# Second-attention steps as one row over all batches, with the first attention's tiles in denser rounds

## What is computed

```python
# layer 1: 16 heads of 16
q, k, v = split(x @ w_in.T + b_in)
att = softmax(einsum('blhd,bmhd->blmh', q, k) / 4, axis=2)
opt = einsum('blmh,blhd->blhd', att, v)          # att is summed over m: only its sums and maxima matter
x = layernorm(x + opt @ w_out.T + b_out)
# layer 2: 4 of 16 heads of 64, chosen per batch
dist = softmax(mean(x @ Wr + br, axis=1))
idx = sort(top_k(dist, 4))
Q, K, V = heads idx of x @ Wq + bq, x @ Wk + bk, x @ Wv + bv
O = softmax(Q K^T / 8) V
x = layernorm(x + O @ Wo + bo)
```

## Time and profile before

| | |
|---|---|
| median of 3 runs | 4088.38 us (4088.38 to 4088.68) |
| the profiled execution | 4086.6 us |
| its span | 4084.8 us |
| PE, DVE, ACT, POOL busy | 89%, 80%, 76%, 41% of the span |
| mean granted TensorE clock | 0.887 of full speed |

### The profile page before, as it was taken

The page is one execution under the profiler, slowest core; times in us unless marked ns, Lnnn a source line. Parts: engine busy times, 40 slices in busy tenths (PEclk is TensorE's granted clock), DMA queues, the critical chain, the costliest instruction groups (busy, mean ns, idle before and its releaser), DMA issues.

```text
span 4084.8 us, 41654 instructions
## 1 busy us (share of the span) xinstructions
PE 3616.2 (89%) x13992; PEld 1329.7 (33%) x13992; DVE 3287.2 (80%) x3352; ACT 3098.1 (76%) x5069; POOL 1662.8 (41%) x1115
## 2 busy tenths in 40 slices
PE   7888888778999999788999999788999999599997
PEld 3233223223333333323333332323333322343443
DVE  7888888988989898888989898888989898543442
ACT  5888888886888889786888889786888889423333
POOL 3122332100445555400445545401445545437776
PEclk7777777678999999878999999778999999799998
DMA  5122221110000000210000000210000000100000
GB/s 159 67 75 67 83 75 62 57 45 16 16 16 19 21 21 26 67 38 16 16 16 19 26 16 26 73 33 16 16 16 25 21 16 19 53 9 1 11 11 11
DMA packets 117192, 142.62 MB, mean 35 GB/s; under 512 B 33394, under 2 KB 100466, under 8 KB 116978
## 3 DMA queue, kind: packets, MB, share of 16 engines
q1 hardware_dynamic: 116978, 139.95, 11.0%
HBM read 89.55 MB, written 50.33 MB: 34 GB/s over the span
## 4 chain that ended last, share of the span: by engine, by line
PE 47%; DVE 29%; ACT 17%; issue 5%; POOL 2%; SPq 1%; DMA 0%; POOLq 0%; DVEq 0%; ACTq 0%
DVE nmax L1083 18%; ACT ps L920 14%; PE ps L796 8%; PE ps L886 8%; PE ps L858 7%; PE ps L761 7%; PE ps L873 7%; DVE smax L1162 6%; PE ps L775 6%; POOL facc L720 2%; PE ps L876 2%; PE ps L769 1%; PE ps L894 1%; ACT probs L990 1%; DVE st L1062 1%
## 5 line engine op out<-in xcount | busy, mean ns | idle before, releaser
L920 ACT ACTIVATE ps<-ps,nmax 128x1024 f32<-128x1024 f32 x2048 | 2233.0, 1094 | 388.4 <-DVE nmax L1083 365.6
L1083 DVE TENSOR_REDUCE nmax<-ps 128x1 f32<-128x1024 f32 x2048 | 2379.4, 1216 | 135.2 <-PE ps L796 122.5
L796 PE MATMUL ps<-stack 96*128 96x512 bf16 x4096 | 1350.6, 436 | 237.0 <-ACT ps L920 149.4
L720 POOL TENSOR_TENSOR facc<-facc,probs 128x1024 f32<-128x1024 f32 x448 | 1051.2, 2346 | 550.9 <-ACT probs L990 528.8
L1162 DVE TENSOR_REDUCE smax<-ps 128x2 f32<-128x1024 f32 x512 | 616.5, 1220 | 261.3 <-PE ps L858 260.9
L796 PEld LDWEIGHTS ps<-stack 96*128 96x128 bf16 x4096 | 298.2, 102 | 1411.0 <-ACT ps L920 939.2
L990 ACT ACTIVATE probs<-ps 128x1024 f32<-128x1024 f32 x512 | 524.0, 1024 | 229.1 <-PE ps L876 227.8
L858 PE MATMUL ps<-fk,fq 64*128 64x512 f32 x2048 | 571.0, 650 | 41.4 <-ACT ps L920 38.1
L873 PE MATMUL ps<-fq,fk 64*128 64x512 f32 x2048 | 545.7, 609 | 29.0 <-ACT ps L920 27.9
L886 PE MATMUL ps<-probs,vals 128*64 128x512 f32 x2048 | 506.9, 608 | 5.0 <-ACT probs L990 4.5
L920 ACT ACTIVATION_READ_ACCUMULATOR ps<-ps,nmax 128x1 f32 x2048 | 417.0, 204 | 0.0
(11 more groups left out here) (117 smaller groups left out, 1985.5 us busy)
## 6 DMA issues: line engine op xcount, KB each, us to landing
stack<-qk_levels SPq DMA_DIRECT2D x768, 64.0 KB, 2.2
qk_levels<-fk SPq DMA_DIRECT2D x64, 384.0 KB, 2.6
probs<-in_L_attn_x SPq DMA_DIRECT2D x16, 512.0 KB, 3.8
res<-in_L_attn_x SPq DMA_DIRECT2D x16, 512.0 KB, 4.0
v_rows<-vals SPq DMA_DIRECT2D x16, 512.0 KB, 2.6
vrows<-v_rows SPq DMA_DIRECT2D x16, 512.0 KB, 3.4
x_rows<-y SPq DMA_DIRECT2D x16, 512.0 KB, 2.9
res<-x_rows SPq DMA_DIRECT2D x16, 512.0 KB, 3.9
```

The costliest lines, as they stand in the source:

```text
L720: pool.tensor_tensor(total, total, probs[:, slot, :], ALU.add).then_inc(facc_ready, 1)
L796: last = pe.matmul(bank(banks[i]), stack[0:SK, hd % 2, 0, t * P:(t + 1) * P], stack[0:SK, hd % 2, 1, col:col + CH], start=True, stop=True)
L920: act.activation(src, src, ACT.Exp, bias=nmax[:, b % 2, half, t, hd:hd + 1], scale=-1.0, accum_out=esum[:, b % 2, half, t, hd:hd + 1]).the ...
L1083: dve.tensor_reduce(nmax[:, b % 2, half, t, hd:hd + 1], two_banks(banks), AX.XY, ALU.min).then_inc(min_ready, 1)
```

## The change

The second attention's steps are numbered over all batches, so that they make one row of rounds: 32 for each batch and 4 behind the last. S of the first group of a batch stands in the same rounds as T and V of the last group of the batch before it. In the last batch those first four rounds' T and V get spots within the seam. A round takes 16 tiles (the pattern `16`) as long as more tiles are left than 12 for each round that remains, less EARLY = 48, and up to 12 otherwise; where tiles are left no more, a letter A is skipped. FK, FV and FQ of the second pair stand in a batch's first four rounds.

What follows from it for the buffers: the last chunk of foT lies in oT and no longer in x1T, and J of two batches on, and R, wait for its users; ACT's eviction of X1 waits for FK, FQ and FV of the batch before, that of FK for T of the last group that reads the same columns of fk, DVE's eviction of FV for V of that group step by step, no longer for its last; the slots of probs are counted over all batches; the norm of a batch's last FO follows the OP norms of the next batch.

The planner's prices are changed too.

```diff
-ROUND = "TSSTAASTAASTAAAVVAAVAVAA"
-LEAD = "SAAAASAAAASAAAASAAAA"
+EARLY = 48
+ROUNDS = {0: "TSSTSTSTVVVV", 12: "AASTAASTSATASTAAAVVAAVAV", 16: "STAASTAASTAASTAAAVAVAAVAAVAA"}
+LEAD = "SAAAASAAAASAAAASAAAATTTTVVVV"
...
+    near = AHEAD / A_TILES
+    rounds = GROUPS * STEPS // BURST
+    behind = STEPS // BURST
+
+    def spot_of(r, part):
+        b, k = divmod(r, rounds)
+        if b == B:
+            return B + (k + part) / rounds
+        return b + near + (1 - near) * (k + part) / rounds
...
-        later = [("FK", b, 1, c) for c in range(NCH)] + [("FQ", b, 1, 0)] + [("FV", b, c) for c in range(NCH)]
-        main += place(later, b + near, (1 - near) * STEPS / (GROUPS + 1) / STEPS)
...
+        later = [u for c in range(NCH) for u in (("FK", b, 1, c), ("FV", b, c))] + [("FQ", b, 1, 0)]
+        late += [(spot_of(b * rounds + behind * (i + 1) / len(later), 0.0), u) for i, u in enumerate(later)]
+        main += [(spot_of(b * rounds + behind * g - behind / 2, 0), ("FQ", b, g % PAIRS, g // PAIRS)) for g in range(2, GROUPS)]
+    given = [AHEAD] * B
+    for r in range(B * rounds + behind):
+        b, k = divmod(r, rounds)
+        if r < behind or b == B - 1 and k < behind:
+            spots = LEAD
+        elif b + 1 < B:
+            spots = ROUNDS[16 if A_TILES - given[b] > 12 * (rounds - k) - EARLY else 12]
+        else:
+            spots = ROUNDS[0]
+        take = {"S": r * BURST, "T": r * BURST - STEPS, "V": r * BURST - STEPS}
+        for i, kind in enumerate(spots):
+            spot = spot_of(r, i / len(spots))
+            if kind == "A":
+                if b + 1 < B and given[b] < A_TILES:
+                    tiles.append((spot, ("A", b + 1, given[b])))
+                    given[b] += 1
+                continue
...
+            if kind != "S" and b == B - 1 and k < behind:
+                spot = b + near * (k + i / len(spots)) / behind
...
-    return [main, scores, products, inputs, tiles]
+    return [main, scores, products, inputs, tiles, late]
...
-            fill(("A", b, j), 0.46, 2, [sp("LS", b, j // HEAD_TILES)] if j % HEAD_TILES == 0 else [], act("A", b, j))
-            unit(dve("A", b, j), 1.155, [pe("A", b, j)])
+            fill(("A", b, j), 0.437, 2, [sp("LS", b, j // HEAD_TILES)] if j % HEAD_TILES == 0 else [], act("A", b, j))
+            unit(dve("A", b, j), 1.135, [pe("A", b, j)])
...
-                fill(("S",) + t, 0.96, 2, [act("FK", b, p, n % NCH), dve("FQ", b, p, c)], dve("S", *t))
-                unit(dve("S", *t), 1.22, [pe("S", *t)] + ([dve("M", *two)] if two and n == 0 else []))
-                fill(("T",) + t, 1.28, 2, [act("M", b, g)] if n == 0 else [], act("T", *t))
+                fill(("S",) + t, 0.86, 2, [act("FK", b, p, n % NCH), dve("FQ", b, p, c)], dve("S", *t))
+                unit(dve("S", *t), 1.135, [pe("S", *t)] + ([dve("M", *two)] if two and n == 0 else []))
+                fill(("T",) + t, 1.17, 2, [act("M", b, g)] if n == 0 else [], act("T", *t))
...
-            events.append((now + (0.18 if n[0] == "PE" else 0.1) + extra[n], 1, r, n))
+            events.append((now + (0.1 if n[0] == "PE" else 0.05) + extra[n], 1, r, n))
...
-        foT = x1T
+        def foT(c):
+            return oT[:, :, :] if c + 1 == NCH else x1T[:, :, c * CH:(c + 1) * CH]
+
...
                     if b:
-                        act.wait_ge(filled, fill_no["FO", b - 1, c])
+                        act.wait_ge(filled, max([fill_no[k, b - 1, p, c] for k in ("FK", "FQ") for p in range(PAIRS)]
+                                                + [fill_no["FV", b - 1, c]]))
+                        if c + 1 < NCH:
+                            act.wait_ge(filled, fill_no["FO", b - 1, c])
...
+                    if b:
+                        act.wait_ge(filled, fill_no["T", b - 1, GROUPS - PAIRS + p, c * TPC + TPC - 1])
...
-                        dve.wait_ge(pv_done, step_no(b - 1, GROUPS - 1, STEPS - 1))
+                        dve.wait_ge(pv_done, step_no(b - 1, GROUPS - 1, c * TPC + TPC - 1))
...
+                    if c + 1 == NCH and b + 1 < B:
+                        dve.wait_ge(filled, fill_no["OP", b + 1, NCH - 1])
```

More of the change, by code:

```diff
@@ L41 @@
 AHEAD = 70
-ROUND = "TSSTAASTAASTAAAVVAAVAVAA"
-LEAD = "SAAAASAAAASAAAASAAAA"
+EARLY = 48
+ROUNDS = {0: "TSSTSTSTVVVV", 12: "AASTAASTSATASTAAAVVAAVAV", 16: "STAASTAASTAASTAAAVAVAAVAAVAA"}
+LEAD = "SAAAASAAAASAAAASAAAATTTTVVVV"
 def work_lists():
-    main, scores, products, inputs, tiles = [], [], [], [], []
+    main, late, scores, products, inputs, tiles = [], [], [], [], [], []
     def place(units, start, span):
@@ new lines, in work_lists @@
+    given = [AHEAD] * B
[15 more added lines that the diff above has]
+                continue
+            n = take[kind]
+            take[kind] += 1
+            if not 0 <= n < B * GROUPS * STEPS:
+                continue
+            at, step = divmod(n, STEPS)
+            if kind != "S" and b == B - 1 and k < behind:
+                spot = b + near * (k + i / len(spots)) / behind
+            unit = (kind, at // GROUPS, at % GROUPS, step)
+            (products if kind == "V" else scores).append((spot, unit))
+            if kind == "T" and step == 0:
+                main.append((spot, ("M",) + unit[1:3]))
+            if kind == "V" and at:
+                was = ((at - 1) // GROUPS, (at - 1) % GROUPS)
+                main += [(spot, ("D",) + was)] * (step == 4) + [(spot, ("R",) + was)] * (step == 8)
+                main += [(spot, ("FO", was[0], was[1] // PAIRS))] * (step == 12 and was[1] % PAIRS == 1)
@@ L115, in work_lists @@
+    for b in range(B - 1):
+        tiles += [(b + 0.9999, ("A", b + 1, j)) for j in range(given[b], A_TILES)]
+    main += [(B + 0.99, ("D", B - 1, GROUPS - 1)), (B + 0.99, ("R", B - 1, GROUPS - 1)), (B + 0.99, ("FO", B - 1, NCH - 1))]
+    for units in (late, scores, products, tiles):
+        units.sort(key=lambda entry: entry[0])
     main.sort(key=lambda entry: entry[0])
-    return [main, scores, products, inputs, tiles]
+    return [main, scores, products, inputs, tiles, late]
 def plan():
@@ L139, in plan @@
     jobs = [t for at, t in lists[3] if t[0] == "XT"]
-    norms = [(k, b, c) for b in range(B) for k in ("OP", "FO") for c in range(NCH)]
+    norms = []
+    for b in range(B):
+        norms += [("OP", b, c) for c in range(NCH)] + [("FO", b - 1, NCH - 1)] * (b > 0)
+        norms += [("FO", b, c) for c in range(NCH - 1)]
+    norms.append(("FO", B - 1, NCH - 1))
     for i, job in enumerate(jobs):
@@ L180, in plan @@
             fill(("X1", b, c), 1.07, 2, [dve("NM", "OP", b, c)], act("X1", b, c))
-            unit(act("X1", b, c), 1.5, [pe("X1", b, c)] + ([pe("FO", b - 1, c)] if b else []))
+            free = []
+            if b:
+                free = [pe(k, b - 1, p, c) for k in ("FK", "FQ") for p in range(PAIRS)] + [pe("FV", b - 1, c), dve("RT", b - 1, 0)]
+                free += [pe("FO", b - 1, c)] if c + 1 < NCH else []
+            unit(act("X1", b, c), 1.5, [pe("X1", b, c)] + free)
         unit(dve("RT", b, 0), 0.2, [act("X1", b, NCH - 1)])
@@ L194, in plan @@
                 unit(dve("FQ", b, p, c), 0.75, [pe("FQ", b, p, c)])
[L195 to L196 removed]
+            free = [pe("V", b - 1, GROUPS - 1, c * TPC + TPC - 1)] if b else []
+            fill(("FV", b, c), 3.72, 2, [sp("LW", b, 2)] + free, dve("FV", b, c))
+            unit(dve("FV", b, c), 1.25, [pe("FV", b, c)])
         for g in range(GROUPS):
@@ L228, in plan @@
                         free = [pool("V", k // (BURSTS - 1) // GROUPS, k // (BURSTS - 1) % GROUPS, k % (BURSTS - 1) + 1)]
-                unit(act("V", b, g, q), 0.62, [pe("V", b, g, q * BURST + BURST - 1)] + free)
+                unit(act("V", b, g, q), 0.5, [pe("V", b, g, q * BURST + BURST - 1)] + free)
                 if q:
@@ L235, in plan @@
             fill(("R", b, g), 0.75, 1, [pool("D", b, g)], dve("R", b, g))
-            unit(dve("R", b, g), 0.68, [pe("R", b, g), pool("V", b, g, BURSTS - 1)])
+            free = [pe("OP", b + 1, NCH - 1)] if b + 1 < B and c + 1 == NCH else []
+            unit(dve("R", b, g), 0.68, [pe("R", b, g), pool("V", b, g, BURSTS - 1)] + free)
     for i, (k, b, c) in enumerate(norms):
@@ L716, in _ @@
                             pool.wait_ge(filled, fill_no["D", (k - 2) // GROUPS, (k - 2) % GROUPS])
-                        pool.tensor_tensor(total, probs[:, slot - 1, :], probs[:, slot, :], ALU.add).then_inc(facc_ready, 1)
+                        pool.tensor_tensor(total, probs[:, before, :], probs[:, slot, :], ALU.add).then_inc(facc_ready, 1)
                     else:
```

38 lines of the change are left out of this document (19 added, 19 removed).

## The result

| | before | after |
|---|---|---|
| median | 4088.38 us (4 runs, 4086.69 to 4088.68) | 4029.87 us (4 runs, 4028.77 to 4036.23) |
| ratio | | 0.9861, 95% interval 0.9844 to 0.9878 |
| profiled execution, its span | 4086.6, 4084.8 us | 4028.95, 4027.1 us |
| PE, DVE, ACT, POOL busy | 89%, 80%, 76%, 41% | 89%, 82%, 77%, 41% |
| mean granted TensorE clock | 0.887 | 0.900 |

The change is faster by 58.5 us (1.4%). Forecast were 100 us; the time lies in the range of 3900 to 4070.

The account below looks back on a forecast made before the run. Steady rounds were taken as PE nearly full (21.3 us), tile-only stages as DVE-bound, seams as latency chains. Gains of 41, 78 and the last seam's reached 107.6, less 7.6: 100 us, forecast 3988 us, range 3900 to 4070.

Parts of the forecast that it names:

- The count of rounds: Second attention: 23 rounds of 16 tiles in batch 0, 27 each in batches 1 and 2, 77 in all.
- A round of 16: Second attention's round with 16 tiles: 24.9 us, the middle of 23.9 and 25.9, with DVE 96% busy.
- the 25.9: Round of 16 tiles if all DVE idle time stays, PSUM banks being too few: 25.9 us, 77 us worse in total.
- Rival D, the clock: Rounds of 16 tiles get a granted clock of 0.77, PE needs 28.6 us, time 4273 us; chance 0.03.
- The rounds of a whole batch: Batches 1 and 2 after their four lead rounds: 23 x 24.9 + 19 + 55 = 647 us.
- A batch: Batches 1 and 2, first OP to first OP: 117 + 112 + 647 = 876 us against 914.8, 39 gained in each.
- The last seam: First OP to first S: chain of 72.7 us, T and V fill idle PE, 8 us added for PE being taken.
- The 7.6 us for D, R and FO: Last group's D, R and FO, moved behind the last seam into PE-bound rounds: 7.6 us lost.
- The planner's prices: Planner's changed costs, touching the part before T of batch 0: worth nothing, with 10 us either way.
- A: The forecast case itself: rounds of 16 tiles at 24.2 to 25.9 us, time 3934 to 4065; chance 0.64.
- What the join's cover is worth: Join, POOL products and waits up to first OP hidden beside four tile-free rounds; batch 0's OP at 1650, 41 us gained.
- full banks (C): Banks run out in rounds of 16 tiles: 27.2 us a round, time 4165, slower than before; chance 0.10.

## Why the prediction was right or wrong

**The count of rounds** held: 23 and 27 rounds of 16; the joins start at 1584.1, 2478.4 and 3375.7, just where the last round with tiles ends.

**A round of 16** was put at 24.9 us and measured 24.8, DVE 96% busy (as forecast); it is the number on which I said all hangs, and it did hold in the twelve rounds shown. That it came so near is in part luck, since 24.9 was the middle of two bounds. The price of PE in it was right, but its row was misread: L876 in the earlier trace rows is two matmuls in 0.22 us, while those of a tile take 0.22 us each (L796 x2 0.60 and x4 1.04 us in the timeline of before).

The idle time of DVE behind PE fell from 2.0 to 1.0 us a round, with the same eight banks. By the Trainium skill's "Perfetto Trace Analysis" (Optimization Strategy) such regular bubbles can mean that PSUM is too small for the next tile, here too few banks; the 25.9 that I had worked out with all of them kept did not come. Rival D, the clock, did not come either: 0.99 in the rounds.

**The rounds of a whole batch** were under-priced. In batch 1 the 24 rounds from T of group 0 to T of group 6, the one of 10 among them, took 601.8 us where I had 592. The same rounds of batch 0 took 589.3. They hold two FO projections, those of batches 1 and 2 three: the last group's D, R and FO of the batch before now stand in them. The forecast counted these, at 7.6 us, behind the last seam alone. Of the 12.5 us between the batches 9.3 are in the first four rounds, where the third FO stands (at 1969.7). That it is the cause is likely and not tested.

**A batch** was put at 876 us and took 894.3 and 890.9. Of the 18 us missing in batch 1, 10 are in the rounds, 5 from T of group 6 to the first OP (62.6 for 57.7, that is the rounds without tiles and the transposes) and 3.5 in the chain of the seam (117.8 for 114.3). The four rounds with FK and FV were right (112.1 for 112).

**The last seam** is the step that failed most. I wrote: "I add 8 us, since a unit of the chain that comes due finds PE taken". It was 27.3, and 17.8 of these were not PE but DVE's small steps waiting for POOL's sums, a term that the forecast did not have. The 9.5 left, with T and V on the chain, are near the 8 that I gave to PE. The 7.6 us for D, R and FO after it were nearly made up by an earlier T of batch 3: 494.5 us to the end against 494.2.

**The planner's prices** were put at nothing, with 10 us either way for the first stage. That stage gained 5.7 us (T of batch 0 at 995.5 for 1001.2), and over the whole changed kernel they are worth 13.5 us. Without them the gain is 43 us (4043.36 against 4086.55 beside it) where 100 were forecast: the prices covered a part of what the structure lacked.

By the spans, 33.2 us were missing in two batches and 19.3 in the last seam, less 2.6 up to seam 1 and 7.3 at the end: 42.6, which is 4027.1 against the forecast span of 3984.8 but for rounding. The time lies in the range, and in that of A, but not by A's working: 4030 would stand there for rounds of 25.4 us. The rounds shown were 24.8, and the range, made wide for them, took up the misses elsewhere. That is luck.

**What the join's cover is worth** was overrated, and the sum did not show it, as it was not made against the alternative. I had 27 us hidden by the early end of the tiles and never asked what the early end costs. By the forecast's own prices (24.9, 21.3, 13.8) a tile added costs 0.90 and a tile taken gives 0.63, so 48 tiles cost 13 us a batch; 27 seemed worth it. It was 15, and to the first S nothing was hidden. The kernel with EARLY = 0 beats the change by 31 us.

**The other side.** Slower was held possible through full banks (C). DVE would have had to stay at 91% or less; it came to 96%.

## What to carry to other kernels

Where two engines are near their bound in the same loop, moving work from one round to another is no even trade: what is added is paid at the price of the engine that becomes full, what is taken is refunded at the price of the one that stays. And before work is put into an idle seam, read which engines' steps on the chain share something with the engine that the new work wakes; here the larger part was not PE, where the room was counted, but POOL, whose sums stretched each small DVE step to their own length.

## What the runs showed of the hardware

DVE steps of 0.16 and 0.40 us (128 x 4 numbers; a scaling of 128 x 256) lasted 2.0 to 2.6 us while POOL added 128 x 1024 numbers from SBUF in 2.35 us, four scalings 7.69 us with three such sums. It went the other way as well: in the kernel with the sums on DVE, a POOL add of 2.35 us took 3.65 us beside DVE's sum of 1.22. DVE's reductions of ps beside the same POOL sums, in the rounds of 16, ran on at their 1.22 us.

Four rounds with S, tiles, FK and FV had a granted clock of 1.00 with T and V in them (PE busy 104.81 of 112.10 us) and 0.85 without (88.67 of 113.50).
